# A fused transformer kernel: the MLP norm's one-token shift done on means and variances instead of on features

## What is computed

```python
def shift_token(t):
    t1, t2 = jnp.split(t, 2, axis=-1)
    t2 = jnp.pad(t2, ((0, 0), (1, 0), (0, 0)))[:, :-1]
    return jnp.concatenate([t1, t2], axis=-1)
...
h = shift_token(x)
mu = h.mean(-1, keepdims=True)
var = h.var(-1, keepdims=True)
h = (h - mu) / jnp.sqrt(var + 1e-05) * lg + lb
h = h @ w1 + b1
a, g = jnp.split(h, 2, axis=-1)
h = a * jax.nn.gelu(g, approximate=False)
x = x + h @ w2 + b2
```

## Time and profile before

| | before |
|---|---|
| median of 3 runs | 1258.32 us (1258.1 to 1260.74) |
| the profiled execution | 1258.88 us, span 1257.1 us |
| TensorE matmul, busy | 1168.3 us, 93% |
| VectorE, busy | 840.2 us, 67% |
| ScalarE, busy | 686.9 us, 55% |
| GpSimd, busy | 587.9 us, 47% |
| mean granted TensorE clock | 0.986 |

### The profile page before, as it was taken

The page is one execution under the profiler, slowest core; times in us unless marked ns, Lnnn a source line. Parts: engine busy times, 40 slices in busy tenths (PEclk is TensorE's granted clock), DMA queues, the critical chain, the costliest instruction groups (busy, mean ns, idle before and its releaser), DMA issues.

```text
span 1257.1 us, 20486 instructions
## 1 busy us (share of the span) xinstructions
PE 1168.3 (93%) x6672; PEld 893.2 (71%) x6672; DVE 840.2 (67%) x2443; ACT 686.9 (55%) x1696; POOL 587.9 (47%) x648
## 2 busy tenths in 40 slices
PE   5899999999999899986689999999999999999888
PEld 4677777777777666755467787777877778777666
DVE  7677777778777365588688657667675776755331
ACT  3667667577676034162366746647465565654721
POOL 2344454444544211147677556564655646563430
PEclk9899999999999999998799999999999999999999
DMA  7112122121223210014000000000001000010010
GB/s 226 44 42 76 35 50 72 38 50 34 51 51 109 77 34 1 1 59 159 1 2 1 1 1 18 1 2 1 1 18 45 28 2 1 2 64 4 1 51 17
DMA packets 31628, 46.11 MB, mean 37 GB/s; under 512 B 4572, under 2 KB 19632, under 8 KB 31536
## 3 DMA queue, kind: packets, MB, share of 16 engines
q1 hardware_dynamic: 31536, 44.98, 12.6%
HBM read 24.00 MB, written 4.19 MB: 22 GB/s over the span
## 4 chain that ended last, share of the span: by engine, by line
PE 53%; issue 20%; POOL 15%; DVE 7%; ACT 4%; DMA 0%; POOLq 0%; DVEq 0%; ACTq 0%
PE psum L1461 33%; POOL probs L625 13%; PE psum L1721 5%; PE psum L1770 4%; PE psum L1755 4%; PE psum L1737 4%; PE psum L1703 2%; ACT hnT_hi L941 1%; DVE stats L994 1%; ACT hnT L941 1%; POOL rn L669 1%; DVE ra L1276 1%; PE psum L1783 1%; DVE rb L1282 1%; DVE xn L1003 1%
## 5 line engine op out<-in xcount | busy, mean ns | idle before, releaser
L625 POOL TENSOR_TENSOR probs<-probs,rden 128x128 f32<-128x128 f32 (+3 forms) x256 | 177.5, 731 | 213.2 <-DVE rden L1055 213.2
L911 ACT ACTIVATE lp<-lp,lneg,rn 128x256 f32<-128x256 f32 (+1 forms) x256 | 143.8, 571 | 17.6 <-DVE lneg L1332 17.4
L780 ACT ACTIVATE probs<-probs,negmax 128x128 f32<-128x128 f32 (+3 forms) x256 | 140.6, 554 | 21.7 <-DVE negmax L1050 21.6
L1043 DVE CUSTOM_DVE_ANT_0 probs<-psum,causal 128x512 f32<-128x512 f32 (+3 forms) x256 | 110.1, 486 | 3.3 <-PE psum L1461 1.4
L669 POOL TENSOR_TENSOR rn<-ss,neg_half 128x8 f32<-128x8 f32 x64 | 107.0, 1671 | 3.8
L1320 DVE CUSTOM_DVE_ANT_0 lp<-psum,local 128x256 f32<-128x256 f32 (+1 forms) x256 | 84.0, 383 | 22.8 <-PE psum L1721 22.8
L660 POOL TENSOR_TENSOR lp<-lp,lrden 128x768 f32<-128x768 f32 x64 | 95.0, 1484 | 0.0
L1461 PE MATMUL psum<-q,k_rest 128*128 128x256 f32 (+2 forms) x256 | 88.9, 358 | 5.4 <-DVE rowmax L1043 3.1
L1527 PE MATMUL psum<-ident,probs 128*128 128x128 f32 x640 | 91.0, 274 | 1.7 <-POOL probs L625 1.6
L1461 PE MATMUL psum<-wqkv_hi,hT_lo 128*128 128x512 f32 x192 | 83.5, 435 | 4.4 <-DVE rb L1282 2.1
L657 POOL TENSOR_TENSOR lp<-lp,lrden 128x128 f32<-128x128 f32 x64 | 26.7, 418 | 128.1 <-DVE lrden L1337 128.1
(11 more groups left out here) (166 smaller groups left out, 3064.4 us busy)
## 6 DMA issues: line engine op xcount, KB each, us to landing
k<-k_round SPq DMA_DIRECT2D x128, 128.0 KB, 2.4
x<-in_x SPq DMA_DIRECT2D x8, 512.0 KB, 6.0
aw<-in_w_quads SPq DMA_DIRECT2D x4, 768.0 KB, 5.1
w_raw<-in_w SPq DMA_DIRECT2D x2, 1364.0 KB, 6.6
ctxT<-in_ctxT SPq DMA_DIRECT2D x4, 512.0 KB, 3.5
x_scratch<-x SPq DMA_DIRECT2D x4, 512.0 KB, 3.7
x<-x_scratch SPq DMA_DIRECT2D x4, 512.0 KB, 5.4
wqkv_raw<-in_wqkv SPq DMA_DIRECT2D x1, 1536.0 KB, 10.0
```

The source lines that it names most:

```text
L625: ins = pool.tensor_tensor(pr, pr, rden[:, j % 2, h, i:i + 1].broadcast_to([P, TRI[i]]), ALU.mult)
L780: ins = act.activation(pr, pr, ACT.Exp, bias=negmax[:, j % 2, h, i:i + 1], scale=ADH ** -0.5, accum_out=den[:, j % 2, h, i:i + 1])
L911: ins = act.activation(pr, pr, ACT.Exp, bias=lneg[:, u % 2, h, w:w + 1], scale=rn[:, m % 2, w, 0, 2 * j + h:2 * j + h + 1], accum_out=lden ...
L1043: ins = dve.tensor_tensor_reduce(probs[:, j % 2, h, TRI_AT[i]:TRI_AT[i + 1]], bank[:, at:at + TRI[i]], causal[:, S - TRI[i]:S], 1.0, -3e38 ...
```

## The change

The token shift is no longer applied to the features. VectorE takes `bn_stats` and `bn_aggr` of both halves of each token's own features (`half`). A small matmul (`moved_on`, item `sh`) moves mean and variance of the second half one token on: eight columns, and six for the carry into the next tile, each with a weight of 128 x 128 cut out of a constant band matrix. Four small VectorE operations combine the two halves into mean and variance, GpSimd takes the reciprocal root as before. A second small matmul (`moved_back`, new item `back`) moves the combined mean and reciprocal root one token back, to where the second half's features lie. `mlp_apply` copies these out of PSUM (`later`), computes what the first token's padded zeros become (`start`), and normalizes both halves from SBUF. `transposed_norm` then shifts for free: the transposition of the second half writes one column further on, its last tile is one token shorter, and column 0 is filled by a matmul of one column. The items `sh` and `back` take PSUM banks 0 and 1 in place of a turn among the `g` banks. All four engines' lists are new; in `closing`, `back` stands between `w20` of step 6 and `apply`. A constant of 128 x 512 takes the place of one of 128 x 256.

```diff
-    shift = np.zeros((P, 2, P), np.float32)
-    shift[:, 0, :] = i == j - 1
-    shift[P - 1, 1, 0] = 1.0
+    band = np.zeros((P, 4 * P), np.float32)
+    band[:, P:2 * P] = 0.5 * np.eye(P)
+    band[0, 3 * P:] = 1.0
...
+        STEP_PE = ("Ta1 Sb2 hnT@-1 k2@1 Sa3 Tb1 hid0@-1 hid1@-1 Tqk1@1 Sb3 AV1 q3@1 hid2@-1 Tqk2@1 "
+                   "hid3@-1 k3@1 hid4@-1 Ta2 hid5@-1 v3@1 hT@2 w20@-1 Tb2 q0@2 Tqk3@1 AV2 Sa0@1 Ta3 "
+                   "k0@2 Sb0@1 w21@-1 q1@2 Tb3 k1@2 Sa1@1 AV3 Sb1@1 Ta0@1 wo0 wo1 Tb0@1 Sa2@1 v0@2 v1@2 "
+                   "Tqk0@2 sh v2@2 AV0@1 back q2@2")
+        STEP_DVE = ("k2 Tb1@-1 Sa3@-1 hid0@-2 Tqk1 fa2@-1 hid1@-2 Sb3@-1 fb2@-1 q3 Tqk2 hid2@-2 fa3@-1 "
+                    "hid3@-2 k3 Ta2@-1 hid4@-2 hid5@-2 weights@1 tab@4 hT@1 Tb2@-1 fb3@-1 w20@-2 Tqk3 "
+                    "q0@1 Sa0 Ta3@-1 Sb0 wparts@-1 fa0 k0@1 Tb3@-1 Sa1 w21@-2 fb0 q1@1 Ta0 Sb1 k1@1 "
+                    "wo0@-1 wo1@-1 Tb0 stats@-1 Sa2 fa1 norm@-1 Tqk0@1 fb1 apply@-1 Ta1 Sb2 hnT@-1 q2@1")
+        STEP_ACT = ("v3 Tqk3 Ta3@-1 AV2@-1 wparts@-1 k0@1 ea0 eb0 q1@1 Tb3@-1 k1@1 AV3@-1 Ta0 ea1 Tb0 "
+                    "v0@1 eb1 Tqk0@1 q2@1 AV0 Ta1 v1@1 hnT@-1 k2@1 v2@1 ea2 Tb1 eb2 hid0@-1 hid1@-1 "
+                    "Tqk1@1 AV1 q3@1 hid2@-1 ea3 hid3@-1 k3@1 Tqk2@1 Ta2 hid4@-1 hid5@-1 weights@2 hT@2 "
+                    "eb3 Tb2 q0@2")
+        STEP_POOL = ("bias q0@3 fb3@1 fa0@2 k0@3 fb0@2 q1@3 norm@1 fa1@2 fb1@2 k1@3 q2@3 k2@3 fa2@2 fb2@2 "
+                     "q3@3 k3@3 fa3@2")
...
             def mlp_rstd(m):
-                pool.wait_ge(f_mv, T * (m + 1))
-                pool.tensor_scalar(rstd[:, 0, :], mv[:, 0, :, 1], LN_EPS, None, ALU.add).then_inc(f_eps, 1)
+                pool.wait_ge(f_var, m + 1)
+                pool.tensor_scalar(rstd[:, 0, :], gap[:, 1, :], LN_EPS, None, ALU.add).then_inc(f_eps, 1)
...
             def mlp_stats(m):
-                for t in range(T):
-                    dve.bn_stats(stats[:, 0, t, 0:6], y[:, m % B, t, 0:P]).then_inc(f_stats, 1)
+                for k in range(2):
+                    for t in range(T):
+                        dve.bn_stats(stats[:, 0, t, 6 * k:6 * k + 6], y[:, m % B, t, k * P:(k + 1) * P])\
+                            .then_inc(f_stats, 1)
+                dve.wait_ge(f_stats, 2 * T * (m + 1))
+                for k in range(2):
+                    for t in range(T):
+                        dve.bn_aggr(half[:, k, t, :], stats[:, 0, t, 6 * k:6 * k + 6]).then_inc(f_half, 1)
 
             def mlp_norm(m):
-                bank = wait_full(dve, plan["sh", m])
-                for t in range(T):
-                    dve.bn_stats(stats[:, 0, t, 6:12], bank[:, t * P:(t + 1) * P]).then_inc(f_stats, 1)
-                dve.wait_ge(f_stats, 2 * T * (m + 1))
-                for t in range(T):
-                    dve.bn_aggr(mv[:, 0, t, :], stats[:, 0, t, :]).then_inc(f_mv, 1)
+                use = plan["sh", m]
+                moved = wait_full(dve, use)[:, 0:2 * T].rearrange("p (t c) -> p t c", c=2)
+                dve.wait_ge(f_half, 2 * T * (m + 1))
+                dve.scalar_tensor_tensor(gap[:, 0, :], half[:, 0, :, 0], 0.5, moved[:, :, 0], ALU.mult, ALU.subtract)\
+                    .then_inc(f_gap, 1)
+                dve.scalar_tensor_tensor(moments[:, :, :].rearrange("p c t -> p t c"), half[:, 0, :, :], 0.5, moved,
+                                         ALU.mult, ALU.add).then_inc(read[use[0]], 1)
+                dve.wait_ge(f_gap, 2 * m + 1)
+                dve.tensor_tensor(gap[:, 1, :], gap[:, 0, :], gap[:, 0, :], ALU.mult).then_inc(f_gap, 1)
+                wait_read(dve, use)
+                dve.wait_ge(f_gap, 2 * m + 2)
+                dve.tensor_tensor(gap[:, 1, :], gap[:, 1, :], moments[:, 1, :], ALU.add).then_inc(f_var, 1)
...
             def mlp_apply(m):
+                use = plan["back", m]
+                bank = wait_full(dve, use)
+                dve.tensor_scalar(later[:, :, :].rearrange("p c t -> p (c t)"), bank[:, 0:2 * T], 2.0, None, ALU.mult)\
+                    .then_inc(f_later, 1)
+                dve.scalar_tensor_tensor(start[:, :], moments[:, 0, 0:1], -1.0, moments[:, 1, 0:1], ALU.mult, ALU.mult)\
+                    .then_inc(read[use[0]], 1)
...
-            def shifted_half(m):
-                for tp in range(2):
-                    wait_read(pe, plan["wo", m, tp])
-                use = plan["sh", m]
-                bank = wait_free(pe, use)
-                mm(bank[:, :].rearrange("p (t e) -> p t e", e=P), shift[:, 0, :], y[:, m % B, :, P:D], start=True,
-                   stop=False, skip_group_check=True)
-                mm(bank[:, P:T * P].rearrange("p (t e) -> p t e", e=P), shift[:, 1, :], y[:, m % B, 0:T - 1, P:D],
-                   start=False, stop=True, skip_group_check=True).then_inc(full[use[0]], 1)
+            def moved_on(m):
+                pe.wait_ge(f_half, 2 * T * (m + 1))
+                use = plan["sh", m]
+                bank = wait_free(pe, use)
+                mm(bank[:, 0:2 * T].rearrange("p (t c) -> p t c", c=2), band[:, P - 1:2 * P - 1], half[:, 1, :, :],
+                   start=True, stop=False, skip_group_check=True)
+                mm(bank[:, 2:2 * T].rearrange("p (t c) -> p t c", c=2), band[:, 2 * P - 1:3 * P - 1],
+                   half[:, 1, 0:T - 1, :], start=False, stop=True, skip_group_check=True).then_inc(full[use[0]], 1)
+
+            def moved_back(m):
+                pe.wait_ge(f_rstd, m + 1)
+                use = plan["back", m]
+                bank = wait_free(pe, use)
+                dst = bank[:, 0:2 * T].rearrange("p (c t) -> p c t", c=2)
+                mm(dst, band[:, P + 1:2 * P + 1], moments[:, :, :], start=True, stop=False, skip_group_check=True)
+                mm(dst[:, :, 0:T - 1], band[:, 1:P + 1], moments[:, :, 1:T], start=False, stop=True,
+                   skip_group_check=True).then_inc(full[use[0]], 1)
...
             def transposed_norm(m):
+                    if e:
+                        mm(bank[:, 0:1], band[:, 3 * P:4 * P], start[:, :], start=True, stop=True)
                     for t in range(T):
-                        ins = pe.transpose(bank[:, t * P:(t + 1) * P], hn[:, t, e * P:(e + 1) * P], ident[:, :])
+                        n = P if t < T - 1 else P - e
+                        ins = pe.transpose(bank[:, t * P + e:t * P + e + n], hn[0:n, t, e * P:(e + 1) * P],
+                                           ident[0:n, 0:n])
```

More of the change, by code:

```diff
@@ L183, in build @@
         b2 = sbt(ctx, "b2", [P, D])
-        shift = sbt(ctx, "shift", [P, 2, P])
+        band = sbt(ctx, "band", [P, 4 * P])
+        half = sbt(ctx, "half", [P, 2, T, 2])
+        moments = sbt(ctx, "moments", [P, 2, T])
+        gap = sbt(ctx, "gap", [P, 2, T])
+        later = sbt(ctx, "later", [P, 2, T])
+        start = sbt(ctx, "start", [P, 1])
         raw = ExitStack()
@@ L262, in build @@
         l_q, l_rn, l_kadd, l_k, l_prob = (sem(n) for n in ("l_q", "l_rn", "l_kadd", "l_k", "l_prob"))
-        f_stats, f_mv, f_hn = (sem(n) for n in ("f_stats", "f_mv", "f_hn"))
+        f_stats, f_half, f_gap, f_var, f_later, f_hn = (
+            sem(n) for n in ("f_stats", "f_half", "f_gap", "f_var", "f_later", "f_hn"))
         f_eps, f_rstd, f_b2 = (sem(n) for n in ("f_eps", "f_rstd", "f_b2"))
@@ L308, in build @@
         UNITS = STEPS * FPAIRS
[L312 to L316, removed]
[3 rows of a table removed]
[L320 to L326, removed]
+        STEP_PE = ("Ta1 Sb2 hnT@-1 k2@1 Sa3 Tb1 hid0@-1 hid1@-1 Tqk1@1 Sb3 AV1 q3@1 hid2@-1 Tqk2@1 "
[3 more added lines that the diff above has]
+        STEP_DVE = ("k2 Tb1@-1 Sa3@-1 hid0@-2 Tqk1 fa2@-1 hid1@-2 Sb3@-1 fb2@-1 q3 Tqk2 hid2@-2 fa3@-1 "
[3 rows of a table added]
+        STEP_ACT = ("v3 Tqk3 Ta3@-1 AV2@-1 wparts@-1 k0@1 ea0 eb0 q1@1 Tb3@-1 k1@1 AV3@-1 Ta0 ea1 Tb0 "
[4 more added lines that the diff above has]
+                     "q3@3 k3@3 fa3@2")
+        MLP = ("stats", "sh", "norm", "back", "apply", "hnT", "hT", "bias")
         def step_items(cycle, m):
@@ L420, in build @@
                 turn(("w1a", *at), "g")
-            if what == "sh":
-                turn(("sh", *at), "g")
+            if what in ("sh", "back"):
+                take((what, *at), ("sh", "back").index(what))
             if what == "Tqk":
@@ L563, in _ @@
             sp.dma_start(b2[:, :], a["b2"][0].partition_broadcast(P)).then_inc(ld_small, 16)
-            sp.dma_start(shift[:, :, :], a["c_shift"]).then_inc(ld_shift, 16)
+            sp.dma_start(band[:, :], a["c_band"]).then_inc(ld_band, 16)
             def layer_wqkv(l, c, dst):
@@ L1373, in mlp_apply @@
                 for t in range(T):
-                    ins = dve.tensor_scalar(hn[:, t, P:D], bank[:, t * P:(t + 1) * P], mv[:, 0, t, 0:1],
-                                            rstd[:, 0, t:t + 1], ALU.subtract, ALU.mult)
-                ins.then_inc(read[use[0]], 1)
```

(11 more changed lines are left out.)

10 lines of the change are left out of this document (4 added, 6 removed), and 5 rows, old and new, of tables (STEP_DVE, closing).

## The result

The changed kernel takes 1282.65 us (1280.08 to 1283.07), the kernel before 1258.39 us: a ratio of 1.0183 over all fast runs, 95% interval 1.0167 to 1.0199 (the two medians alone: 1.0193). Forecast was 1255.7. The change makes the kernel 1.8% slower.

A forecast was written before the change was run, and what follows sets the result against it. TensorE, busy 93% of the span, was taken to bound the kernel, except at its two ends; 1258.88 - 6.7 + 1.2 + 0.9 + 2.0 = 1256.3 us profiled, or 1255.7 us median, range 1250.0 to 1262.5.

The forecast's parts named there:

- Part 1: TensorE in each step: 1.51 us of shift removed, ten small matmul records added at 1.0 us, between 0.3 and 1.7.
- third rival: Tiny matmuls on TensorE nearly free, 0.03 us a record, a step saves 1.8 us: 1250.0 us; chance 0.13.
- Part 2: VectorE's norm work per step 5.5 us after, 4.5 before, hidden by TensorE's work; GpSimd's part stays.
- Part 3: Full steps, wo of step 0 to wo of step 6: 1.1 us saved a step, -6.7 us over six.
- the replay: New engine lists laid against each other with profiled item lengths; no wait over 0.2 us found in a full step.
- the second: Norm's chain becomes TensorE's wait in every step, hops 0.2 us dearer: about 1263 us, half of that 1259; chance 0.22.
- Part 4: Start of the small transformer, up to wo of step 0: 673.3 in place of 672.1, +1.2 us, between -2.6 and +4.
- Part 5: Last two steps, without later projections to fill in: +0.9 us in step 6, +2.0 us in step 7.
- first rival: Clock falls in one of the longer waits at start or end: one fall 1258.4 us, two 1261; chance 0.25.

The follow-up runs named there:

- free_port: Changed kernel with GpSimd's scaling of the local probabilities of each step's second head pair cut to one column (computation left out): 1268.44 us, ratio 1.0069.
- pool_first: Changed kernel with GpSimd's softmax scaling of the first head (fa1) moved ahead of the norm's power: 1273.67 us, ratio 1.0121.
- order_only: Kernel before, with its own norm, in the new loop orders without the item back, sh in bank 0: 1276.09 us, ratio 1.0148.
- after_fill: Changed kernel with unread identity transpositions ahead of the last two sh, the last AV and the last hid0: 1282.11 us, ratio 1.0170.
- old_start: Changed kernel with all four engines' lists as before up to wo of step 0, the new ones from there: 1274.39 us, ratio 1.0136.
- before_fill: Kernel before with unread identity transpositions ahead of the second Sb (80), the last AV (24) and the last hid0 (32): 1260.31 us, ratio 0.9998.
- combo2: Changed kernel with old lists up to wo of step 0, fa1 ahead of norm, idle matmuls in three end waits: 1265.27 us, ratio 1.0043.

## Why the prediction was wrong

**Part 1, TensorE's work: right.** 1.05 us for the ten records, 1.0 forecast. The rule of about 25 ns between small matmuls (the Trainium skill, TensorE: Matmul & The Clock Gate, section "Wait — 56ns, not 53.3ns?") is not reached here: a record takes 0.09 to 0.12 us. The third rival, 0.03 us a record, is out.

**Part 2, VectorE: the term that was mis-sized.** I costed the eight normalizings at 0.28 us each, "by the pace of the rows". That pace was taken in a pause of GpSimd. In the new order four of them take 3.31 us. The trace of before had a hint, in the two forms' shortest, median and longest duration (ns; by tile):

```profile
L1374 DVE TENSOR_SCALAR hn<-psum,mv,rstd x32: 397/402/414, 686.2 to 1214.4; 128x128 f32<-128x128 f32 x32
L1378 DVE TENSOR_SCALAR hn<-y,mv,rstd x32: 332/340/486, 687.5 to 1215.5; 128x128 f32<-128x128 f32 x32
```

The form out of SBUF is the one that varies. And I had laid GpSimd's own list beside the others only for who waits on whom.

**Part 3, the full step: the replay right up to `apply`, and wrong by that term.** `sh` at 12.3 us (forecast 12.1), `back` at 15.9 (15.8), both without a wait. `hnT`, with 0.7 us to spare in the forecast, waits 1.56. Over the six steps 9.7 in place of -6.7, a miss of 16.4 us: the waits for `hn` 9.4 (shown by `free_port` and `pool_first`), those for `lmax` and `lv` about 3.2, and 0.64 x 6 = 3.8 of seams (measured as what is left in the step, only partly placed), which I had not in the sum because I took each piece of TensorE's work to cost the same whatever stands next to it. That the 0.62 us wait goes came true. Of the rivals this was the second, the norm's chain as TensorE's wait: its sign and place were right, its mechanism (dearer hops) was not, and its price, up to 1.1 us a step, too low.

**Part 4, the start: waits right, their price wrong.** TensorE went on at 614.9 (615.7 forecast), and the waits that the replay gave came where it gave them, 2.19 and 1.39 us at `Tqk`, 2.76 at `AV3`. But `wo` of step 0 is at 678.4 and not at 673.3. I take the 5.1 us to be the clock's loss in 640 to 644 and 670 to 678, behind those same waits, which sums to 5.1. For it speaks that of the six kernels with the new order up to there the one with the smallest such sum from 626 us on, 1.7 us (`order_only`), has the earliest `wo`, 674.6, and the one with the largest, 7.2 (`after_fill`), the latest, 682.1. `old_start` shows that the new order brought the loss; that it is the clock alone is not shown, and `before_fill` warns that a faster TensorE might have met other waits there.

**Part 5, the end: as the start.** The wait before `sh` of step 7 is 3.21 us (3.35 forecast). In step 6 `hid0` starts 24.1 us after `wo` (22.1 forecast), with the clock at 0.57 from 1179 to 1187. `sh` waits 2.64 us there (2.4 forecast), but not for `half`, as I had it: that was through at 1172.9, and the last 0.7 us were bank 0, which VectorE still read. The end takes 7.4 us more in place of 2.9, and up to 10.3 - 3.4 = 6.9 of them are clock; filling three of the four long waits took 5.8 us off (`combo2` against `pool_first`), `after_fill`, less its misplaced fillings, and `combo2` end in 111 to 112 us. This is the first rival, which I gave one fall or two, 2.7 us each. From 626 us on it came in six places, five more than before; I had asked the question only of the two longest new waits.

Together 16.4 + 5.1 + 4.5 = 26 us, the whole of the miss in the profiled execution (1282.28 us for 1256.3). So two steps of the prediction failed: the price of four normalizings, at 1.1 us where they took 3.31 beside GpSimd, and the longer waits at both ends, which I priced by their length alone. That the price of the seams brings the steps' sum out so exactly is arithmetic: they are what is left there.

## What to carry to other kernels

A duration from a trace belongs to what the neighbours did at that moment: before VectorE work is moved, look what GpSimd does at the new place. Here `tensor_scalar` from SBUF to SBUF had to be counted by the end of GpSimd's running instruction, with a PSUM operand by its own pace. A new wait on TensorE has a second price beside its length. Waits of 2.6 to 3.5 us were here mostly followed by 3 to 7 us in which the clock was 0.50 and the same matmuls took up to twice as long (scores 2.08 us for 1.13); that counts where TensorE is what the time waits for. Where such a wait can't be avoided, idle matmuls in it gave the clock back (0.26% of the time here), but only inside the wait and into a bank that was already free.
